# Edge scores of a graph layer added into their table cells, the edge count beside them

## The reference, cut to what matters

```python
xl = (x @ W_l).reshape(N, HEADS, HEAD_DIM)      # 625 x 4 x 64
xr = (x @ W_r).reshape(N, HEADS, HEAD_DIM)
e = xl[src] + xr[dst]
e = jnp.where(e >= 0, e, 0.2 * e)
score = jnp.einsum('ehd,hd->eh', e, att)        # 4 words an edge
m = segment_max(score, dst); ex = jnp.exp(score - m[dst])
alpha = ex / (segment_sum(ex, dst)[dst] + 1e-16)
agg = segment_sum(alpha[:, :, None] * xl[src], dst)
```

## Time and profile before

| | |
|---|---|
| median of three runs | 1161.55 us (1156.02, 1161.55, 1164.46) |
| profiled execution, first to last instruction | 1154.3 us; no time around it is given |
| mean granted clock of PE | 0.912 of full speed |
| PE, DVE, ACT, POOL busy | 948.9, 858.0, 466.5, 463.7 us |
| first scatter turn on POOL | from 68.6 us |
| last scatter issued, tables loaded from | 515.9 and 518.9 us |
| five tables taken by DVE | 531.9 to 582 us |

### The profile page before, as it was taken

The page is one execution under the profiler, slowest core; times in us unless marked ns, Lnnn a source line. Parts: engine busy times, 40 slices in busy tenths (PEclk is TensorE's granted clock), DMA queues, the critical chain, the costliest instruction groups (busy, mean ns, idle before and its releaser), DMA issues.

```text
span 1154.3 us, 19240 instructions
## 1 busy us (share of the span) xinstructions
PE 948.9 (82%) x6532; PEld 829.5 (72%) x6532; DVE 858.0 (74%) x1953; ACT 466.5 (40%) x795; POOL 463.7 (40%) x374
## 2 busy tenths in 40 slices
PE   4586998879989998983835999985898588599996
PEld 2566886768978887853734999974588377589885
DVE  5659468869777978997987888776688765866635
ACT  1453755467858686616621111110253053212120
POOL 2448888877777877860001222250000000211104
PEclk9888999789999999997865999997999698699999
DMA  8962222323222232209704999983000000588883
GB/s 295 276 194 64 56 69 68 74 48 73 63 62 62 63 77 47 48 11 247 189 1 137 324 316 333 316 299 116 0 1 1 1 1 1 211 307 304 297 317 91
DMA packets 57946, 157.58 MB, mean 137 GB/s; under 512 B 23797, under 2 KB 32938, under 8 KB 49618
## 3 DMA queue, kind: packets, MB, share of 16 engines
q1 hardware_dynamic: 26830, 125.59, 33.3%
q0 software_dynamic: 25056, 24.10, 9.3%
q10 hardware_dynamic: 5992, 7.04, 1.7%
HBM read 136.50 MB, written 19.86 MB: 135 GB/s over the span
## 4 chain that ended last, share of the span: by engine, by line
PE 33%; DMA 24%; DVE 17%; POOL 12%; issue 10%; SPq 3%; POOLq 0%; ACT 0%; DVEq 0%; ACTq 0%
DMA pair_scores<-sc_ring,idx_ring 13%; PE bank L775 11%; PE bank L786 6%; POOL pair_scores L2153 5%; POOL arena L2143 5%; DMA arena<-pair_scores 4%; PE bank L544 3%; PE bank L708 2%; POOL arena L2208 2%; PE bank L496 2%; SPq L2232 2%; DMA arena<-slot_y,sloti 2%; DMA arena<-in_exp 1%; PE bank L697 1%; PE bank L874 1%
## 5 line engine op out<-in xcount | busy, mean ns | idle before, releaser
L2198 POOL DMA_INDIRECT arena<-row_tab,ids x42 | 57.7, 1373 | 493.7 <-DVE ids L1563 486.6
L2153 POOL DMA_INDIRECT pair_scores<-sc_ring,idx_ring x160 | 210.2, 1314 | 60.3 <-issue 43.4
L2143 POOL DMA_INDIRECT arena<-xl_tab,idx_ring x120 | 157.6, 1313 | 81.3 <-issue 31.7
L775 PE MATMUL bank<-arena 128*128 128x128 f32 x1480 | 180.8, 280 | 3.2 <-DMA arena<-in_exp 3.0
L775 PEld LDWEIGHTS bank<-arena 128*128 128x128 f32 x1480 | 175.0, 197 | 5.3 <-DMA arena<-in_exp 4.1
L1888 ACT ACTIVATE arena<-fmaps,node_neg 125x875 f32<-125x875 int32 x100 | 100.1, 1022 | 34.5 <-PE bank L544 34.5
L786 PE MATMUL bank<-arena 128*128 128x256 f32 (+1 forms) x404 | 97.6, 384 | 1.2 <-DMA arena<-in_exp0o 1.2
L1892 ACT ACTIVATE late_ohT<-arena 125x875 fp32r<-125x875 f32 x100 | 90.6, 926 | 0.0
L2021 ACT ACTIVATE arena<-bank 128x512 f32<-128x512 f32 (+2 forms) x76 | 34.4, 453 | 126.6 <-PE bank L775 126.5
L544 PE MATMUL bank<-late_hi,late_ohT 125*125 125x256 f32 x500 | 83.7, 298 | 0.6 <-DVE arena L1035 0.6
L786 PEld LDWEIGHTS bank<-arena 128*128 128x128 f32 (+1 forms) x404 | 72.1, 190 | 14.9 <-issue 6.0
(11 more groups left out here) (357 smaller groups left out, 2017.4 us busy)
## 6 DMA issues: line engine op xcount, KB each, us to landing
arena<-in_exp SPq DMA_DIRECT2D x25, 1024.0 KB, 7.1
arena<-in_exp SPq DMA_DIRECT2D x17, 1386.0 KB, 6.1
arena<-in_exp0o SPq DMA_DIRECT2D x25, 512.0 KB, 7.3
pair_scores<-cnt SPq DMA_DIRECT2D x10, 1093.8 KB
arena<-in_exp1o SPq DMA_DIRECT2D x17, 640.0 KB
fmaps<-in_rows SPq DMA_DIRECT2D x20, 437.5 KB, 3.8
arena<-pair_scores SPq DMA_DIRECT2D x7, 1093.8 KB
slot_y<-arena ACTq DMA_DIRECT2D x34, 128.0 KB, 6.4
```

The costliest lines, as they stand in the source:

```text
L775: mm = pe.matmul(banks[1 + 2 * q + buf][0:rows, i * SLOTS:(i + 1) * SLOTS], w_in(s, q, k, m, rows), xsT[:, s, k, :], start=(k == 0), stop= ...
L2143: p.indirect_dma_start(out=gat[:, b % 2, 0, j * D:(j + 1) * D], out_offset=None, in_=xl_tab, in_offset=bass.IndirectOffsetOnAxis(ap=idx_ri ...
L2153: p.indirect_dma_start(out=pair_scores[which], in_=sc_ring[:, b % 2, j, :], in_offset=None, out_offset=bass.IndirectOffsetOnAxis(ap=idx_ri ...
L2198: p.indirect_dma_start(out=xs[:, q, :], out_offset=None, in_=tab, in_offset=bass.IndirectOffsetOnAxis(ap=ids[:, q, :], axis=0))\
```

## The change

The scatters add instead of writing, five words a row: four scores and a count of one. The tables start from zeros with 1e-15 in the fifth word, and 125 spare cells stand behind them. Since an adding DMA must not name a cell twice, DVE compares each column's cells with all 125 cells of the column (`count_twins`) and decides (`place_twins`, `write_cells`): the first of several equal edges carries the scores and the count times their number, and the others go to spare cells with a factor of zero. For this the cell numbers are turned by PE, stored, and loaded per group as rows on all partitions by SP (`load_cells`).

The one-hots and products that counted edges, their reads and their sums are gone. `LATE` is 8 in place of 12, and late groups make columns 2, 3 and 4 and fetch two. The sums of late groups alternate between two sets of banks (`row_bank`). ACT makes four of the five tiles of late one-hots and copies the sums of the made columns times 0.2 (`fifth`); DVE makes the fifth tile (`hot_tile`) and takes the maximum of the copy and the bank. At the end POOL adds the two halves of each table; DVE takes the reciprocal of the count, multiplies the scores by it and masks empty cells; ACT takes the logarithm, table by table. For the second layer ACT scales `cnt` by 8 once, and DVE's mask and scaling there are gone.

The core of the diff (what counted edges is only removed, and is left out):

```diff
-LATE = 12
-BEHIND = 4
-
-
-PIECES = [(0, 1), (3, 4), (2,)]
+LATE = 8
+
+
+PIECES = [(0, 1), (2, 3), (4,)]
 NP = len(PIECES)
-MADE = PIECES[1]
-FETCHED = [j for piece in PIECES if piece != MADE for j in piece]
-FETCH_AFTER = (0, 2, 3)
-COUNTED = [(0, 1), (2,), (3, 4)]
+MADE = PIECES[1] + PIECES[2]
+FETCHED = list(PIECES[0])
+FETCH_AFTER = (0, 2)
...
-        pair_scores = [nc.dram_tensor(f"pair_scores{i}", [N * NC, H], F32).ap() for i in range(2)]
+        pair_scores = [nc.dram_tensor(f"pair_scores{i}", [N * NC + P, HR], F32).ap() for i in range(2)]
+        cell_rows = nc.dram_tensor("cell_rows", [EC, P], F32).ap()
...
+        def row_bank(late, s, r):
+
+
+            return banks[r if late and s == 1 else T + r]
...
+            def count_twins(g, b, ch):
+
+
+                s = b % 2
+                dve.wait_ge(sem(f"cells{s}"), g * 8 + (16 - 8 * s))
+                for j in range(G):
+                    ch.note(v.scalar_tensor_tensor(twin_junk[j], cell_row[0:P, s, j * P:(j + 1) * P],
+                                                   cellf[:, bass.ds(g * G + j, 1)], twin_weight[:, :], ALU.is_equal,
+                                                   ALU.mult, accum_out=twins[:, j:j + 1]))
+
+            def place_twins(g, b, ch):
+
+
+                ch.fence()
+                ch.note(v.scalar_tensor_tensor(cell_kept[:, :], twins[:, :], EARLIER, cellf[:, bass.ds(g * G, G)],
+                                               ALU.is_lt, ALU.mult))
+                ch.note(v.scalar_tensor_tensor(cell_spare[:, :], twins[:, :], EARLIER,
+                                               spare_cell[:, 0:1].to_broadcast([P, G]), ALU.is_ge, ALU.mult))
+                v.scalar_tensor_tensor(times[:, b % 4, :], twins[:, :], EARLIER, twins[:, :], ALU.is_lt, ALU.mult)\
+                    .then_inc(sem("twins_met"), 1)
+                ch.fence()
+                dve.wait_ge(sem("twins_met"), g + 1)
+
+            def write_cells(g, b):
+                v.tensor_tensor(idx_ring[:, b % 4, 1, :], cell_kept[:, :], cell_spare[:, :], ALU.add)
...
+            def head_sums(ch, s, b, rows):
+
+
+                ch.link(v.tensor_reduce(sums[:, :, 0:H], rows.rearrange("p (g h c) -> p g h c", g=G, h=H), AX.X, ALU.add))
+                v.tensor_tensor(sc_ring[:, s, :, :], sums[:, :, :],
+                                times[:, b % 4, :].unsqueeze(2).to_broadcast([P, G, HR]), ALU.mult)\
+                    .then_inc(sem("scored"), 1)
...
+            def hot_tile(g, b):
...
+                dve.wait_ge(sem(f"rows{s}"), g * 8 + (16 - 8 * s))
+                dve.wait_ge(sem("z_made"), g * NP - NP)
+                v.tensor_scalar(hot[1, s][:, T - 1, :], edge_row[1, s][0:P, :], node_f[:, T - 1:T], None, ALU.is_equal)\
+                    .then_inc(sem("tile_hot"), 1)
...
+            def late_group(g, b, ch):
 
                 s = b % 2
                 fetched = gat[:, s, 0, :]
+                more = lambda n: not (isinstance(g, int) and g + n >= NG)
+
+                def made_row(r):
+                    dve.wait_ge(sem("fifth"), g * 2 + (r - 2 * LATE))
+                    return v.tensor_tensor(part_of(scored_rows, r), part_of(fetched, r), row_sums(r, 1, s), ALU.max)
+
+                n = 16 * len(FETCHED)
+                dve.wait_ge(sem(f"gathered{s}"), g * (n // 2) + (8 * LATE * G + n - n // 2 * (LATE + s)))
                 dve.wait_ge(sem("z_made"), g * NP + 1)
+                piece = part_of(fetched, 0)
+                v.tensor_tensor(piece, piece, row_sums(0, 1, s), ALU.add).then_inc(sem("z_read"), 1)
+                if more(1):
+                    hot_tile(g + 1, b + 1)
+                dve.wait_ge(sem("z_read"), g * NP + 1)
+                ch.note(leaky(fetched, FETCHED))
+                if more(2):
+                    count_twins(g + 2, b + 2, ch)
+                made_row(1).then_inc(sem("z_read"), 1)
+                ch.note(made_row(2))
+                dve.wait_ge(sem("z_read"), g * NP + 2)
                 ch.fence()
+                weigh(scored_rows, att_late).then_inc(sem("z_read"), 1)
+                if more(2):
+                    place_twins(g + 2, b + 2, ch)
                 dve.wait_ge(sem("z_read"), g * NP + NP)
                 for w in range(2):
                     after(dve, sem(f"scattered{w}"), scores_written(w, g - 1, 0, b - 1))
+                head_sums(ch, s, b, scored_rows)
+                if more(2):
+                    write_cells(g + 2, b + 2)
                     copy_indices(g + 2, b + 2)
...
+            blank_cells = cnt[:, :, :].rearrange("p t n -> p (t n)").rearrange("p (n h) -> p n h", h=HR)
+            own.link(v.memset(cnt[:, :, :], 0.0))
+            v.memset(blank_cells[:, :, H:HR], BLANK_COUNT).then_inc(sem("blank"), 1)
+            v.memset(sums[:, :, :], 1.0)
...
-                dve.wait_ge(sem(f"sdense{m}"), 32 * len(PARTS))
-                first, second = (sdense[q] for q in SDENSE[m])
-                v.tensor_tensor(first, first, second, ALU.max).then_inc(sem("merged"), 1)
                 dve.wait_ge(sem("merged"), m + 1)
+                pairs = sdense[SDENSE[m][0]]
+                own.link(v.reciprocal(rcount, pairs[:, :, H]))
+                own.note(v.tensor_tensor(pairs[:, :, 0:H], pairs[:, :, 0:H],
+                                         rcount.unsqueeze(2).to_broadcast([P, N, H]), ALU.mult))
                 dve.wait_ge(sem("log_met"), m + 1)
+                own.note(v.tensor_scalar(no_edge, cnt[:, m, :], -1.0, -BIG, ALU.is_lt, ALU.mult))
+                own.fence()
+                own.link(v.tensor_tensor(cnt[:, m, :], cnt[:, m, :], no_edge, ALU.add))
                 for h in range(H):
                     i = m * H + h
                     after(dve, sem("l0_prob"), i - 2)
-                    v.tensor_tensor_reduce(masked[:, i % 3, :], first[:, 0:N, h], cnt[:, m, :], -1.0, -LOWEST,
+                    v.tensor_tensor_reduce(masked[:, i % 3, :], pairs[:, :, h], cnt[:, m, :], -1.0, -LOWEST,
                                            ALU.add, ALU.min, rneg[:, i:i + 1]).then_inc(sem("l0_max"), 1)
 
             def average(m):
...
+            def fifth(g, s, r):
+
+
+                act.wait_ge(sem("z_made"), g * NP + (r + 1))
+                at = slice(PIECES[r][0] * D, (PIECES[r][-1] + 1) * D)
+                a.activation(gat[:, s, 0, at], row_bank(1, s, r)[0:P, 0:len(PIECES[r]) * D], ACT.Copy, scale=0.2)\
+                    .then_inc(sem("fifth"), 1)
+
+            def late_group(g, b):
+
+                s, ahead = b % 2, (b + 1) % 2
+                if isinstance(g, int) and g + 1 >= NG:
+                    fifth(g, s, 1)
+                    fifth(g, s, 2)
+                    return
+                rows_ready(g + 1, ahead)
+                apart_tile(g + 1, ahead, 1, 0)
+                apart_tile(g + 1, ahead, 1, 1)
+                hot_tile(g + 1, ahead, 1, 0)
+                apart_tile(g + 1, ahead, 1, 2)
+                hot_tile(g + 1, ahead, 1, 1)
+                apart_tile(g + 1, ahead, 1, 3)
+                fifth(g, s, 1)
+                hot_tile(g + 1, ahead, 1, 2)
+                hot_tile(g + 1, ahead, 1, 3).then_inc(sem("rows_hot"), 1)
+                fifth(g, s, 2)
...
+            def log_counts(m):
+                act.wait_ge(sem("merged"), m + 1)
+                a.activation(cnt[:, m, :], sdense[SDENSE[m][0]][:, :, H], ACT.Ln).then_inc(sem("log_met"), 1)
...
-                pool.sem_inc(sem("pool_turn"), 1)
+                pool.sem_inc(sem("turn"), 1)
                 p.indirect_dma_start(
                     out=pair_scores[which], in_=sc_ring[:, b % 2, j, :], in_offset=None,
-                    out_offset=bass.IndirectOffsetOnAxis(ap=idx_ring[:, b % 4, 2, j:j + 1], axis=0))\
+                    out_offset=bass.IndirectOffsetOnAxis(ap=idx_ring[:, b % 4, 1, j:j + 1], axis=0),
+                    compute_op=ALU.add)\
                     .then_inc(sem(f"scattered{which}"), 16)
 
...
+            for m in range(T):
+                first, second = (sdense[q][:, :, :].rearrange("p n h -> p (n h)") for q in SDENSE[m])
+                pool.wait_ge(sem(f"sdense{m}"), 32 * len(PARTS))
+                p.tensor_tensor(first, first, second, ALU.add).then_inc(sem("merged"), 1)
...
+            def load_cells(g, s):
+
+                after(sp, sem("twins_met"), g - 1)
+                sp.sem_inc(sem("turn"), 1)
+                sp.dma_start(cell_row[:, s, :], cell_rows.rearrange("(g j) p -> g (j p)", j=G)[bass.ds(g, 1), :]
+                             .rearrange("a n -> (a n)").partition_broadcast(128)).then_inc(sem(f"cells{s}"), 16)
 
 
             def edge_rows(g, s, late):
 
                 after(sp, sem("rows_hot"), g - 1)
+                if late and not (isinstance(g, int) and g < LATE + 2):
+                    sp.sem_inc(sem("turn"), 1)
+                    sp.wait_ge(sem("tile_hot"), g - (LATE + 1))
+                    sp.sem_inc(sem("turn"), 1)
                 n = ROWS if late else G * P
```

(21 more changed lines are left out.)

384 lines of the change are left out of this document (125 added, 259 removed).

## The result

| | before | changed |
|---|---|---|
| median (runs) | 1163.01 us (1164.46, 1161.55, 1156.02, 1166.98) | 1279.36 us (1278.66, 1280.05, 1281.28, 1276.38) |
| profiled span | 1154.3 us | 1276.9 us |
| granted clock of PE | 0.912 | 0.837 |

The ratio is 1.100, with a 95% interval of 1.0956 to 1.1045: the change makes the kernel 10% slower. The forecast was 1172 and its range ended at 1214.

The account below looks back on a forecast made before the run. POOL's issuing of indirect DMAs was taken to bound the edge groups, DVE the tables. From the profiled 1154.3 us, scatters ending 21 earlier and tables +32 gave 1165.3, plus 7.25 carried over: 1172 us, range 1138 to 1214.

Parts of the forecast that it names:

- Start, +5: Before the first scatter turn: larger blank tables and cell-row loads cost 5 us, between 0 and 10.
- Fewer issues: Edge groups: four early turns become late ones; late turns issue seven DMAs for eight, at 1.63 us each, 11.4 us.
- the wait on the table: Late groups: same-table scatters two slots (3.26 us) apart wait for a 4.2 us landing, making the period 12.37 us.
- the ring of ACT, PE and DVE: Late groups: hand-overs among these engines take over 12.4 us, leaving POOL's saved issues idle; up to 1200 us, chance 0.05.
- Landing, 4.2: Edge groups: an adding scatter lands 4.2 us after its issue starts, against 3.5 for a plain one.
- Issue, +0: Edge groups: POOL issues an adding scatter in the usual 1.20 us; up to +0.6 kept for the range.
- Rival B: Edge groups: adding is dear, by landings over 4.9 us or longer issue; 1194 to 1248 us, chance 0.23.
- Tables, +32: Tables' stage: larger loads +3, POOL's first addition +7, DVE's passes +5.2 for each of five tables, less 3.7 of waits.
- +3 for the last landings: End of the scatters: the last ten land at 4.2 us in place of 3.5, in about four pairs, +2.8 us.
- rival C: Tables' stage: four POOL additions hold up DVE's passes beside them, +14 to +28 us, 1186 to 1200; chance 0.1.
- Later, 0: Second layer: DVE's dropped mask and scaling and ACT's one scaling lie beside PE's products, 0 us.
- the most hopeful case of the change: Whole kernel: accumulating is free, and reciprocal or POOL's addition is quick too, down to 1131 us; rival's whole chance 0.27.

Follow-up runs that it names:

- e1: The changed kernel with scatters that write their five words in place of adding them: 1201.31 us, ratio 1.0355.
- e11: The kernel before the change with scatters and fetches of 128 rows in place of 125: 1110.53 us, ratio 0.9528.
- e4: The changed kernel with the cell rows of groups 2 and 3 loaded ahead of the second blank table: 1275.36 us, ratio 1.099.
- e14: The kernel before the change with scatters of 128 rows and fetches left at 125: 1136.44 us, ratio 0.9772.

## Why the prediction was wrong

**What bounds the kernel.** Right. POOL bounds the edge groups before and after; with writing scatters the waits for the table and, in the early turns, for DVE take a part (e1), and PE takes over only when both kinds of DMA are cheap in the kernel before (e11).

**Start, +5: mis-sized.** It is +21.0. The forecast took a blank table for 1.22 MB. That is one of its five pieces; a table is 6.25 MB, so both grew by 3.1 MB and not by 0.61. With that size its own sum, 3.1 and 0.64 MB at 293 GB/s, gives 13 us, beyond the 10 given as the upper end. The table's own lateness was 17.4. The rest is the loads for groups 2 and 3: the forecast took them as hidden, but they stood behind the table, and DVE's comparison for group 2 stands ahead of its sum for group 0 (3.6 us, e4).

**Fewer issues, and the wait on the table: right in their sum, and that by luck.** With writing scatters (e1) the edge stretch is 28 us shorter than before; the forecast's terms without the start make 29. But the six early turns took 18.3 us each in place of the 16.33 taken, since POOL waited for DVE in them, which is 12 us more, and what follows them was 11 us shorter than forecast: the late period was 12.03 for 12.37. The forecast's own formula gives plain scatters 11.43 to 11.67, so it missed there too. The rival that the ring of ACT, PE and DVE holds the period over 12.4 fell.

**Landing, 4.2: near in size, wrong in its reason.** It is 3.7 in the median, and 3.0 when writing. The forecast had put 0.7 on top of a plain landing of 3.5 for reading the cell; 0.7 is also the difference found, but all of it is the longer issue. After the issue an adding scatter lands as soon as a writing one, 1.7 and 1.8 us later. This agrees with the rule of the Trainium skill weighed in the prediction (DMA: Bandwidth & Descriptors, Specifications). Nor did the landing decide anything: with issues of 1.98 us two scatters and their gaps are 4.6 us long, and POOL waited for no landing beyond its usual gap.

**Issue, +0: the step that failed.** "I take 0, and keep 0.6 for the range": it is +0.78, outside the kept end. The argument was that a fetch of 64 times the bytes is issued in 1.23 us. It held for bytes (one word or five, 1.98), but bytes were not what was added. Adding costs POOL 0.6 to 0.8 us whatever the width, and it made 76 us in the stretch (e1). Rival B had this mechanism, with 1248 for +0.6 and a chance of 0.23.

**Tables, +32 and +3 for the last landings: +54.** Reciprocal 4.07 for 4.0, product 2.76, mask 0.48 (the forecast wrote 0.42, its row has 0.48), addition 0.81 and score passes came as forecast; POOL's addition is 5.72, between 3.5 and the 7 taken. The rest is rival C: 21.6 us in four stretched passes, forecast at 14 to 28 with a chance of 0.1. It was set beside the forecast as an alternative, when it comes on top of any other case. The parts close: the first table is taken 9.5 us later after the last scatter (13 forecast), DVE's passes are 5.4 us longer a table, 4.2 us of waits are gone, and with 21.6 that makes 54.

**Later, 0: right** (-0.6).

So the terms that failed are issue (+76), start (+16) and C (+22). They make 114 us, where the forecast's 1165 and the span's 1277 are 112 apart; what is left over is -2, over all the other terms.

## What to carry to other kernels

Where one engine's issuing sets the pace, an edit that changes the kind of its instructions must be priced by that kind before anything else: 160 issues turned a small unknown into the whole result. Look at the number of rows of every indirect DMA: here padding 125 rows to 128 was worth 4.7%, some 54 us, in the kernel before, more than the most hopeful case of the change (1131). And work given to an idle POOL is not free for DVE when both read memory: the passes to look at are those that run beside it.

## What the runs showed of the hardware that was not expected

- POOL's issue of an indirect DMA goes with its rows divided by their largest divisor up to 16: 0.98 us for 128 writing rows and 1.20 for 125; adding, 1.57 for 128, 1.98 for 125, 2.2 for 124, and 4.70 for 127.
- A fetch of 128 rows landed 2.8 us after the start of its issue, one of 125 rows 4.3 us (e11 and the kernel before).
- The packets of POOL's queue fell too where scatters add: 82,400 in the changed kernel, 38,880 with scatters of 128 rows, 31,840 with the fetches too. They are not the price of the issue: 128 writing rows in e14 left the 25,056 of before as they were, and the issue fell from 1.20 to 0.99 us.
- The width of an adding row, 4 to 20 bytes, did not change its issue (1.98 us).
- A pass of DVE over four words took 5.64 us beside POOL's addition of two arrays; the 4.07 us reciprocal was not touched by any of four forms of POOL passes.
